# Three token chains laid out anew behind the main loop of a cross-attention, linear-attention and expert kernel

## The chip, the cores and the metric

The kernel runs on one core of one Trainium2 chip. The metric is the device time of one execution in microseconds. An execution under the profiler has its own time, and a span (first to last instruction) a little shorter than that.

## What is computed

The reference has three residual stages over x (8 x 64 tokens of 256), all in float32:

```python
x = x + xattn(layernorm(x), ctx)   # 16 heads of 64 over 1601 context rows, layernorm inside, tanh gate
x = x + attn(layernorm(x))         # linear attention, 8 heads of 64, batches of 64 tokens
x = x + ffn(layernorm(x))          # router, top 2 of 8 experts, 256 -> 1024 (relu) -> 256
# attn:
q = softmax(q, axis=-2) * SCALE    # over the 64 features of a head
k = softmax(k, axis=-1)
context = einsum('bhdn,bhen->bhde', k, v)
out = einsum('bhde,bhdn->bhen', context, q)
```

(In the code the 64 tokens of a batch are regrouped by the reshape of the reference, so that both softmaxes are over groups of 64 within a token's 512 columns.)

## The kernel before, in words

The 512 tokens are 4 tiles of 128 (MT). Every engine has its own queue with a program written out by hand; semaphores tie them together. The work runs in "slots" numbered k. Slots 0 to 207 (NSLOT = 16 groups x 13 context tiles) are the cross-attention: in slot k TensorE makes the scores of tile k (`scores`, L1491), and `times_context` (L1515, 12 matmuls) of tile k - 19. VectorE subtracts the maximum from tile k - 17 (L1073) and makes the low part of tile k - 18 (L1098); ScalarE takes exponents and high parts (L839). The last tiles of that pipeline run out in slots 208 to 226, and the last attention group is written to `oT` in slot 230. `DRAIN` is 231.

Behind that each token tile m goes through a "chain" (one function `chain(m, o)` for each engine, L882, L1145, L1601) of 16 steps o. On TensorE: 0 output product O (`wout_sb`), 2 transpose T1, 3 K, 4 Q, 5 V, 6 and 7 transposes KT and QT, 8 and 9 the head contexts C0 and C1, 10 OT, 11 Y, 13 transpose T2, 14 router product R. On VectorE: 0 adds and statistics (to `eps1`), 1 ln1, 3 K minus its maximum, 4 the same for Q and the normalisation of k, 6 the normalisation of q, 9 cbd, 11 adds and statistics (to `eps2`), 12 ln2, 13 lnT_lo, 14 the routing group (logit, top, tdiff, index, topf, two onehot, cnt), 15 the gates. ScalarE copies and exponentiates between them. POOL makes each `rstd` (L732), in an order written out at L767.

`CHAIN_AT` gives the slot in which a chain starts. In each slot, on each engine, the odd chains come first, then the slot's own work, then the even chains (L1752 to L1758, the same on the others). Chains 0 and 2 use PSUM bank `trp[0]`, chain 1 `trp[1]`, chain 3 a bank of `scp`. The buffers of a chain (`ln_out`, `lnT`, `ke`, `qe`, `kn`, `v_sb`, `cbd`) exist twice, set m % 2; so chain 2 waits for chain 0's logit, chain 3 for chain 1's (L1621).

The chains that aren't done at `SPREAD` = 239 leave only chain 3, whose steps 8 to 14 are set by `LAST` between the tiles of the first expert: n = 0 to 7 are `h_tile(0, n)` (6 matmuls each, L1711), n = 8 to 15 `y_tile(0, n - 8)` (4 matmuls each, L1726). After n = 1 come the ranks of chains 0 to 2 (`first_ranks`, L1738), at the end `last_rank`, which needs chain 3's cnt; then the second half of the tokens. ScalarE writes the high parts of the expert weights (`high_weights`, in quarters: two of w1, two of w2), POOL the low parts (`low_weights`, L735, L743): `w_ready` counts them; the first h tile needs two of them, the first y tile four. SP loads the raw weights, the first two experts when the last `times_context` is done.

Of the kernel before, what the change touches and what calls it, by code (L numbers as in the profile page):

```python
# [125 lines left out]
def build(nc, x, ctx_n, ctx_t, gamma, beta, w_q, w_kt, w_v, w_out, b_out, gate, Wq, Wk, Wv, Wo, bo,  # L126
          W_router, b_router, W1, b1, W2, b2, out):
    with ExitStack() as es:
# [91 lines left out]
        lqT = ke  # L220
        lo_T = qe[:].rearrange("p r (t q) -> p r t q", q=P)
# [74 lines left out]
        w2_sp = tsb("w2_sp", [P, 2, FT, 2 * D], F32R)  # L296
# [139 lines left out]
        def chain_bank(m):  # L436

            return [trp[0], trp[1], trp[0], scp[:, MT - 1, :]][m]
# [13 lines left out]
        def w_quarter(s, part):  # L452

            if part < DT:
                return w1_raw[:, s, part, :], w1_hi[:, s, part, :], w1_lo[:, s, part, :]
            fs = slice((part - DT) * FT // 2, (part - DT + 1) * FT // 2)
            return w2_raw[:, s, fs, :], w2_sp[:, s, fs, 0:D], w2_sp[:, s, fs, D:2 * D]
# [225 lines left out]
        def _(pool):  # L683
# [83 lines left out]
            for m, which in ((0, 1), (1, 1), (0, 2), (2, 1), (1, 2), (3, 1), (2, 2)):  # L767
                chain_rstd(m, which)
# [26 lines left out]
        def _(act):  # L795
# [86 lines left out]
            def chain(m, o):  # L882

                r, bank = m % 2, chain_bank(m)

                def after_pe(name):
                    act.wait_ge(chain_pe[m], PE_NO[name])

                def after_dve(name):
                    act.wait_ge(chain_dve[m], DVE_NO[name])  # L890

                if o == 2:
                    after_pe("T1")
                    act.activation(lnT[:, r, :, :], bank[:, 0:D].rearrange("p (t q) -> p t q", q=P),
                                   ACT.Copy).then_inc(chain_act[m], 1)
                elif o == 4:
                    after_dve("ksub")
                    act.activation(ke[:, r, :, :], ke[:, r, :, :], ACT.Exp).then_inc(chain_act[m], 1)
                elif o == 5:
                    after_dve("qsub")  # L900
                    act.activation(qe[:, r, :], qe[:, r, :], ACT.Exp).then_inc(chain_act[m], 1)
                    after_pe("V")
                    act.activation(v_sb[:, r, :], bank, ACT.Copy).then_inc(chain_act[m], 1)
                elif o == 6:
                    after_pe("KT")
                    act.activation(kn[:, r, :], bank, ACT.Copy).then_inc(chain_act[m], 1)
                elif o == 7:
                    after_pe("QT")
                    act.activation(lqT[:, r, :, :].rearrange("p t q -> p (t q)"), bank,
                                   ACT.Copy).then_inc(chain_act[m], 1)  # L910
                elif o == 10:
                    after_pe("OT")
                    act.activation(lo_T[:, r, :, :].rearrange("p t q -> p (t q)"), bank,
                                   ACT.Copy).then_inc(chain_act[m], 1)
                elif o == 13:
                    after_pe("T2")
                    ps = bank[:, 0:D].rearrange("p (t q) -> p t q", q=P)
                    if m == 0:
                        act.wait_ge(split_ok, len(JOBS))
                    act.activation(lnT_hi[:, :, m * P:(m + 1) * P], ps, ACT.Copy).then_inc(chain_act[m], 1)  # L920
                    act.activation(lnT[:, r, :, :], ps, ACT.Copy).then_inc(chain_act[m], 1)
# [84 lines left out]
        def _(dve):  # L1006
# [138 lines left out]
            def chain(m, o):  # L1145

                r, bank = m % 2, chain_bank(m)
# [22 lines left out]
                def normalised(which):  # L1170
                    dve.wait_ge(chain_pool[m], which)
                    dst = ln_out[:, r, :] if which == 1 else xln[:, m, :]
                    done(dve.tensor_scalar(dst, x_m, mv[:, m, 0:1], rstd[:, m:m + 1], ALU.subtract, ALU.mult))
# [18 lines left out]
                ke_m = ke[:, r, :, :].rearrange("p t q -> p (t q)")  # L1192
                if o == 0:
                    after_pe("O")
                    done(dve.tensor_tensor(ln_out[:, r, :], bank[:, 0:D], bout_b[:], ALU.add))
                    after("o+b")
                    done(dve.scalar_tensor_tensor(out=x_m, in0=ln_out[:, r, :], scalar=tg[:, 1:2], in1=x_m,
# [7 lines left out]
                elif o == 4:  # L1205
                    after_pe("Q")
                    minus_row_max(1, qe[:, r, :], "qmax")
                    after_act("exp_k")
                    normalise(0, ke_m, "ksum", "krec")
                elif o == 6:  # L1210
                    after_act("exp_q")
                    normalise(1, qe[:, r, :], "qsum", "qrec")
                elif o == 9:
                    after_pe("C1")
                    done(dve.tensor_scalar(cbd[:, r, :, :, :], bank.rearrange("p (b t e) -> p b t e", b=2, e=LD),
                                           float(LD) ** -0.5, None, ALU.mult))
                elif o == 11:
                    after_pe("Y")
                    done(dve.tensor_tensor(ln_out[:, r, :], bank[:, 0:D], bo_b[:], ALU.add))
                    after("y+b")  # L1220
                    done(dve.tensor_tensor(x_m, x_m, ln_out[:, r, :], ALU.add))
# [224 lines left out]
        def _(pe):  # L1446
# [154 lines left out]
            def chain(m, o):  # L1601

                r, bank = m % 2, chain_bank(m)
# [11 lines left out]
                if o == 0:  # L1615
                    pe.wait_ge(o_ok, 4 * (m + 1))
                    if m < 2:
                        pe.wait_ge(out_ok, NSLOT)
                        pe.wait_ge(max_ok, NSLOT)
                    else:  # L1620
                        pe.wait_ge(chain_dve[m - 2], DVE_NO["logit"])  # L1621
# [4 lines left out]
                elif o == 2:  # L1626
                    after_dve("ln1")
                    for dt in range(DT):
                        ins = pe.transpose(bank[:, dt * P:(dt + 1) * P], ln_out[:, r, dt * P:(dt + 1) * P], ident[:])
                    done(ins)  # L1630
                elif o == 3:
# [3 lines left out]
                    for t in range(HP):  # L1635
                        for dt in range(DT):
                            ins = pe.matmul(bank[:, t * P:(t + 1) * P], lw_sb[:, 1, dt, t * P:(t + 1) * P],
                                            lnT[:, r, dt, :], start=dt == 0, stop=dt == DT - 1)
                    done(ins)
                elif o in (4, 5):  # L1640
                    after_dve("ksub" if o == 4 else "qsub")
                    for dt in range(DT):
                        ins = pe.matmul(bank, lnT[:, r, dt, :], lw_sb[:, 0 if o == 4 else 2, dt, :],
                                        start=dt == 0, stop=dt == DT - 1)
                    done(ins)
                elif o == 6:
                    after_act("v")
                    after_dve("kmul")
                    for t in range(HP):
                        ins = pe.transpose(bank[:, t * P:(t + 1) * P], ke[:, r, t, :], ident[:])  # L1650
                    done(ins)
                elif o == 7:
                    after_act("kn")
                    after_dve("qmul")
                    for t in range(HP):
                        ins = pe.transpose(bank[:, t * P:(t + 1) * P], qe[:, r, t * P:(t + 1) * P], ident[:])
                    done(ins)
                elif o in (8, 9):
# [7 lines left out]
                    for t in range(HP):  # L1666
                        for hr in head_rows:
                            h = slice(t * P + hr.start, t * P + hr.stop)
                            n0 = (b * HP + t) * LD
                            ins = pe.matmul(bank[hr, n0:n0 + LD], kn[rows, r, h], v_sb[rows, r, h],  # L1670
                                            start=True, stop=True)
                    done(ins)
                elif o == 10:
                    after_dve("cbd")
                    for t in range(HP):
                        for b in range(2):
                            for hr in head_rows:
                                ins = pe.matmul(bank[hr, t * P + b * Q:t * P + (b + 1) * Q], cbd[hr, r, b, t, :],
                                                lqT[hr, r, t, b * Q:(b + 1) * Q], start=True, stop=True)
                    done(ins)  # L1680
                elif o == 11:
                    after_act("lo_T")
                    for t in range(HP):
                        ins = pe.matmul(bank[:, 0:D], lo_T[:, r, t, :], wo_sb[:, t, :],
# [7 lines left out]
                elif o == 14:  # L1692
                    after_act("lnT2")
                    after_dve("lnT_lo")
                    for dt in range(DT):
                        ins = pe.matmul(bank[:, 0:NE], lnT[:, r, dt, :], wr_sb[:, dt, :],
# [19 lines left out]
            def y_tile(p, f):  # L1716
# [7 lines left out]
                for m in tiles(p):  # L1724
                    ms = slice(m * P, (m + 1) * P)
                    pe.matmul(scp[:, m, :], h_hi[:, f, ms], w2_sp[:, 0, f, :], start=f == 0, stop=False)  # L1726
                    ins = pe.matmul(scp[:, m, 0:D], h_lo[:, f, ms], w2_sp[:, 0, f, 0:D],
# [98 lines left out]
            def y_z(z, f):  # L1826
# [12 lines left out]
                for a in range(2):  # L1839
                    b = 2 * (z % 2) + a  # L1840
                    ms = slice(a * P, (a + 1) * P)
                    pe.matmul(scp[:, b, :], h_hi[:, f, ms], w2_sp[:, s, f, :], start=f == 0, stop=False)  # L1842
                    ins = pe.matmul(scp[:, b, 0:D], h_lo[:, f, ms], w2_sp[:, s, f, 0:D],  # L1843
# [24 lines left out]
            for a in range(2):  # L1868
                b = 2 * (z % 2) + a
                ms = slice(a * P, (a + 1) * P)  # L1870
                for f in range(FT):
                    if a == 0:
                        pe.wait_ge(hl_ok, (z + 2) * FT + (f + 1))
                    pe.matmul(scp[:, b, :], h_hi[:, f, ms], w2_sp[:, s, f, :], start=f == 0, stop=False)
                    ins = pe.matmul(scp[:, b, 0:D], h_lo[:, f, ms], w2_sp[:, s, f, 0:D],
# [68 lines left out]
```

## Time and profile before

| | us |
|---|---|
| median of 3 runs | 940.38 (939.36 to 943.42) |
| the profiled execution | 947.82 |
| its span | 946.0 |
| PE busy | 902.2 (95%) |
| DVE busy | 700.6 (74%) |
| POOL busy | 603.3 (64%) |
| ACT busy | 520.4 (55%) |

PE is TensorE's matmuls, DVE VectorE, ACT ScalarE, POOL GpSimd. Busy time is the time in which the engine has an instruction under way. The slots from 208 on begin near 663 us of the span, the first h tile at 768.7, the last rank at 794.2. The clock column of a row is TensorE's granted clock as a share of full speed. Durations of matmuls overlap: the start of one matmul comes before the end of the one before, so the cost of a row of matmuls is read from start to start.

### The profile page before, as it was taken

How to read it: one execution, taken by the hardware profiler on the slowest of the kernel's cores; microseconds unless marked ns; L12 is line 12 of the kernel's file. 1: busy time of each engine (PE TensorE's matmuls, PEld its weight loads, DVE VectorE, ACT ScalarE, POOL GpSimd, SP SyncE). 2: the span in 40 equal slices, each digit the busy share in tenths (PEclk: the TensorE clock that was granted, in tenths of full speed). 3: DMA queues.
4: the chain of work that ended last, by engine and by line, in shares of the span. 5: the costliest groups of instructions: out<-in, count | busy, mean ns of one | idle time of the engine just before them, and what ended most of it. 6: DMA issues, size and time to landing. Idle time of an engine off the chain costs nothing.

```text
span 946.0 us, 17135 instructions
## 1 busy us (share of the span) xinstructions
PE 902.2 (95%) x6228; PEld 787.7 (83%) x6228; DVE 700.6 (74%) x1223; ACT 520.4 (55%) x915; POOL 603.3 (64%) x647
## 2 busy tenths in 40 slices
PE   6999999999999999999999999999999889999997
PEld 3567888888888888888888888888878668998996
DVE  4659787887978878797786879777586576866765
ACT  2547565565655665565565655655354233565662
POOL 5739778857957876895795789471001056677773
PEclk9999999999999999999999999999999978999998
DMA  5872222312322331332231122110200521466632
GB/s 166 258 261 74 76 78 83 95 43 81 89 55 79 88 86 56 81 85 59 77 84 48 46 60 65 40 37 2 67 1 2 178 87 51 138 219 208 225 123 78
DMA packets 102802, 88.23 MB, mean 93 GB/s; under 512 B 10032, under 2 KB 98112, under 8 KB 102720
## 3 DMA queue, kind: packets, MB, share of 16 engines
q1 hardware_dynamic: 101952, 85.04, 29.9%
q0 software_dynamic: 768, 2.10, 0.7%
q8 instruction: 51, 0.84, 0.4%
q14 instruction: 31, 0.25, 0.1%
HBM read 67.46 MB, written 19.66 MB: 92 GB/s over the span
## 4 chain that ended last, share of the span: by engine, by line
PE 82%; DVE 11%; ACT 3%; issue 2%; POOL 1%; DMA 1%; SPq 0%; POOLq 0%; DVEq 0%; ACTq 0%
PE sps L1510 29%; PE scp L1528 10%; PE scp L1530 9%; PE scp L1529 9%; PE scp L1842 3%; DVE u_sb L1108 2%; PE sps L1821 2%; PE wps L1821 2%; PE wps L1555 2%; PE scp L1843 2%; DVE st L1073 1%; PE sps L1623 1%; PE scp L1478 1%; PE sps L1464 1%; DVE pt_lo L1098 1%
## 5 line engine op out<-in xcount | busy, mean ns | idle before, releaser
L1528 PE MATMUL scp<-cn,pt_hi 128*128 128x258 f32 (+1 forms) x832 | 239.4, 288 | 4.4 <-DVE pt_lo L1098 3.7
L1529 PE MATMUL scp<-cn,pt_hi 128*128 128x256 f32 (+1 forms) x832 | 234.9, 282 | 0.0
L1530 PE MATMUL scp<-cn,pt_lo 128*128 128x258 f32 (+1 forms) x832 | 234.7, 282 | 0.0
L837 ACT ACTIVATE st<-sps 128x512 f32<-128x512 f32 (+1 forms) x208 | 123.4, 593 | 146.5 <-PE sps L1510 145.8
L1098 DVE TENSOR_TENSOR pt_lo<-st,pt_hi 128x512 fp32r<-128x512 f32 (+1 forms) x208 | 195.3, 939 | 6.6 <-ACT pt_hi L846 6.6
L1073 DVE TENSOR_TENSOR st<-st,mbc 128x512 f32<-128x512 f32 (+1 forms) x208 | 158.1, 760 | 39.0 <-ACT mbc L860 38.4
L843 ACT ACTIVATE st<-st 128x512 f32<-128x512 f32 (+1 forms) x208 | 130.3, 627 | 89.2 <-DVE st L1073 88.6
L1510 PE MATMUL sps<-qk_hi,ct_hi 128*128 128x512 f32 (+1 forms) x416 | 168.2, 404 | 11.1 <-DVE cmax L1084 6.6
L1528 PEld LDWEIGHTS scp<-cn,pt_hi 128*128 128x128 f32 (+1 forms) x832 | 156.9, 189 | 14.9 <-DVE pt_lo L1098 6.6
L1510 PE MATMUL sps<-qk_hi,ct_lo 128*128 128x512 f32 (+1 forms) x416 | 164.2, 395 | 0.0
L1510 PE MATMUL sps<-qk_lo,ct_hi 128*128 128x512 f32 (+1 forms) x416 | 163.4, 393 | 0.0
L1529 PEld LDWEIGHTS scp<-cn,pt_hi 128*128 128x128 f32 (+1 forms) x832 | 157.2, 189 | 7.4 <-issue 0.2
L1084 DVE TENSOR_TENSOR cmax<-cmax,sps 128x512 f32<-128x512 f32 x192 | 130.6, 680 | 37.3 <-ACT st L837 37.2
L1530 PEld LDWEIGHTS scp<-cn,pt_lo 128*128 128x128 f32 (+1 forms) x832 | 157.7, 190 | 0.0
L707 POOL TENSOR_TENSOR cn<-raw,zero 128x256 fp32r<-128x256 f32 (+1 forms) x104 | 79.9, 768 | 118.1 <-PE scp L1530 111.9
L846 ACT ACTIVATE pt_hi<-st 128x512 fp32r<-128x512 f32 (+1 forms) x208 | 131.5, 632 | 6.6
L709 POOL TENSOR_TENSOR cn<-raw,cn 128x256 fp32r<-128x256 f32 (+1 forms) x104 | 100.3, 964 | 8.2
L1510 PEld LDWEIGHTS sps<-qk_hi,ct_hi 128*128 128x128 f32 (+1 forms) x416 | 76.6, 184 | 30.9 <-issue 15.8
L709 POOL TENSOR_TENSOR ct_lo<-raw,ct_hi 128x256 fp32r<-128x256 f32 (+1 forms) x104 | 92.9, 893 | 8.1
L1510 PEld LDWEIGHTS sps<-qk_hi,ct_lo 128*128 128x128 f32 (+1 forms) x416 | 76.4, 184 | 20.3
L707 POOL TENSOR_TENSOR ct_hi<-raw,zero 128x256 fp32r<-128x256 f32 (+1 forms) x104 | 85.5, 822 | 11.8 <-DMA raw<-ctx_t 11.8
L1510 PEld LDWEIGHTS sps<-qk_lo,ct_hi 128*128 128x128 f32 (+1 forms) x416 | 76.6, 184 | 10.3
(291 smaller groups left out, 1496.3 us busy)
## 6 DMA issues: line engine op xcount, KB each, us to landing
w_raw<-W SPq DMA_DIRECT2D x22, 1024.0 KB, 7.6
raw<-ctx_t SPq DMA_DIRECT2D x96, 128.0 KB, 2.2
raw<-ctx_n SPq DMA_DIRECT2D x96, 128.0 KB, 2.0
raw<-qk_scratch SPq DMA_DIRECT2D x56, 128.0 KB, 2.0
xg_scratch<-zrow SPq DMA_DIRECT2D x32, 128.0 KB, 2.3
yg_scratch<-zrow SPq DMA_DIRECT2D x32, 128.0 KB, 2.3
qk_scratch<-stage_b SPq DMA_DIRECT2D x4, 896.0 KB, 4.8
qk_scratch<-stage_a SPq DMA_DIRECT2D x4, 896.0 KB, 4.5
```

The source lines that it names most:

```text
L707: pool.tensor_tensor(hi, src, z.broadcast_to(tuple(src.shape)), ALU.add).then_inc(split_hi, 1)
L709: pool.tensor_tensor(lo, src, hi.bitcast(F32), ALU.subtract).then_inc(done, 1)
L837: act.activation(st[0:rows(j), par, j, :], sps[0:rows(j), u % 2, :], ACT.Copy).then_inc(out_ok, 1)
L843: act.activation(p, p, ACT.Exp).then_inc(exp_ok, 1)
L846: act.activation(pt_hi[0:rows(j), r, :], p, ACT.Copy).then_inc(hi_ok, 1)
L1073: dve.tensor_tensor(p, p, mbc[0:rows(j), par, :], ALU.subtract).then_inc(sub_ok, 1)
L1084: dve.tensor_tensor(m, m, src, ALU.max).then_inc(max_ok, 1)
L1098: dve.tensor_tensor(pt_lo[0:rows(j), r, :], st[0:rows(j), par, j, :], pt_hi[0:rows(j), r, :].bitcast(F32), ALU.subtract).then_inc(lo_ok, 1)
L1510: ins = pe.matmul(sps[0:rows(j), u % 2, :], a[:, dt, cols], v[:, par, dt, :], start=c == 0, stop=c == 5)
L1528: pe.matmul(scp[:, t, 0:D + 2], hi, cn[0:rows(j), j, 0:D + 2], start=j == 0, stop=False)
L1529: pe.matmul(scp[:, t, 0:D], hi, cn[0:rows(j), j, D + 2:CNW], start=False, stop=False)
L1530: ins = pe.matmul(scp[:, t, 0:D + 2], lo, cn[0:rows(j), j, 0:D + 2], start=False, stop=j == SJ - 1)
```

## The change

Chain 1 starts at slot 223 in place of 213, chain 2 at 224 in place of 223; chain 3 stays at 231. `SPREAD` becomes 240, so step 8 of chain 3 (C0) runs in slot 239, ahead of the first h tile, and no longer behind the second. Chain 3 gets a third set of buffers, laid where `w2_sp` of expert 1 lies; chain 2 keeps set 0. ScalarE writes the high parts of that expert's `w2` later, and those of its `w1` at n = 4 and 12 in place of 2 and 6. `W_HI_AT` moves from 234 to 235 with SPREAD.

```diff
-CHAIN_AT = [NSLOT, NSLOT + 5, NSLOT + 15, DRAIN]
+CHAIN_AT = [NSLOT, NSLOT + 15, NSLOT + 16, DRAIN]
+CHAIN_SET = [0, 1, 0, 2]
 CHAIN_LEN = 16
 SPREAD = CHAIN_AT[2] + CHAIN_LEN
-LAST = dict(zip((1, 2, 4, 5, 6, 11, 13), range(SPREAD - DRAIN, CHAIN_LEN - 1)))
+LAST = dict(zip((2, 4, 5, 6, 11, 13), range(SPREAD - DRAIN, CHAIN_LEN - 1)))
...
-        w2_sp = tsb("w2_sp", [P, 2, FT, 2 * D], F32R)
+        w2_sp = [tsb("w2_sp0", [P, FT, 2 * D], F32R)]
+        third = ExitStack()
...
+        ln_out3 = third_sb("ln_out3", [P, D])
+        lnT3 = third_sb("lnT3", [P, DT, P])
+        ke3 = third_sb("ke3", [P, HP, P])
+        qe3 = third_sb("qe3", [P, HID])
+        kn3 = third_sb("kn3", [P, HID])
+        v_sb3 = third_sb("v_sb3", [P, HID])
+        cbd3 = third_sb("cbd3", [P, 2, HP, LD])
+        third.close()
+        w2_sp.append(tsb("w2_sp1", [P, FT, 2 * D], F32R))
+
+        def three(two, last):
+            return [two[:, 0], two[:, 1], last[:]]
...
-            for m, which in ((0, 1), (1, 1), (0, 2), (2, 1), (1, 2), (3, 1), (2, 2)):
+            for m, which in ((0, 1), (0, 2), (1, 1), (2, 1), (3, 1), (1, 2), (2, 2)):
                 chain_rstd(m, which)
...
-                r, bank = m % 2, chain_bank(m)
+                r, bank = CHAIN_SET[m], chain_bank(m)
...
-                if n % 4 == 2:
-                    high_weights(1, n // 4)
+                if n in (4, 12):
+                    high_weights(1, n // 8)
             chain(MT - 1, 15)
+            act.wait_ge(chain_pe[MT - 1], PE_NO["R"])
             for f in range(FT):
                 relu(1, f)
+                if f in (2, 5):
+                    high_weights(1, 2 + f // 3)
...
                     if m < 2:
                         pe.wait_ge(out_ok, NSLOT)
                         pe.wait_ge(max_ok, NSLOT)
-                    else:
-                        pe.wait_ge(chain_dve[m - 2], DVE_NO["logit"])
+                    elif m == 2:
+                        pe.wait_ge(chain_dve[0], DVE_NO["logit"])
```

The other lines of the diff only replace a buffer's index `[:, r]` by the list of three, `ke_of[r]` and so on, and `w2_sp[:, s]` by `w2_sp[s]`.

## Rows read from the trace of the kernel before

**Rows 1.** Busy time by stretch: us, PE, PEld, DVE, ACT, POOL, clock, DMA, GB/s

```profile
664.00:723.00 59.00, 55.42 (x484) 47.64 (x483) 41.73 (x90) 27.77 (x50) 2.82 (x3) 1.00 0.07 25
...
745.00:768.70 23.70, 17.75 (x130) 13.26 (x129) 12.40 (x30) 8.36 (x13) 8.70 (x13) 0.89 0.05 16
...
757.00:766.90 9.90, 6.77 (x26) 3.63 (x24) 8.06 (x15) 4.53 (x8) 6.35 (x10) 1.00 0.00 0
```

**Rows 2.** PE's order of time: start, us, line, tiles, count, idle before and releaser

```profile
718.20 0.51 PE L1696 MATMUL sps<-wr_sb,lnT 128*128 128x8 f32 x4
...
721.26 3.62 PE L1623 MATMUL sps<-wout_sb,oT 128*128 128x256 f32 x16
...
733.06 1.95 PE L1637 MATMUL sps<-lnT,lw_sb 128*128 128x128 f32 x16
...
740.08 1.98 PE L1643 MATMUL sps<-lw_sb,lnT 128*128 128x512 f32 x4 [1.51 <-DVE qe L1181]
...
745.00 3.62 PE L1623 MATMUL scp<-wout_sb,oT 128*128 128x256 f32 x16
748.55 1.43 PE L1670 MATMUL sps<-v_sb,kn 64*64 64x64 f32 x32
...
752.20 1.15 PE L1678 MATMUL sps<-ke,cbd 64*64 64x64 f32 x32 [0.16 <-DVE cbd L1215]
753.28 3.68 PE L1637 MATMUL scp<-lnT,lw_sb 128*128 128x128 f32 x16
756.79 1.89 PE L1684 MATMUL sps<-wo_sb,qe 128*128 128x256 f32 x8
```

**Rows 3.** DVE's order of time, 737 to 774 us: step starts, routing group, gates

```profile
737.39 0.36 DVE L1244 TENSOR_SCALAR onehot<-eidx,topf 128x8 f32<-128x8 f32 x2
...
738.61 0.69 DVE L1179 TENSOR_REDUCE lmax<-sps 128x8 f32<-128x512 f32 x1 [0.65 <-PE sps L1643]
...
741.50 0.15 DVE L1249 TENSOR_SCALAR tsum<-texp 128x1 f32<-128x1 f32 x1
...
748.66 0.42 DVE L1195 TENSOR_TENSOR ln_out<-scp,bout_b 128x256 f32<-128x256 f32 x1 [3.93 <-PE scp L1623]
...
750.32 0.15 DVE L1168 TENSOR_SCALAR mv<-mv 128x1 f32<-128x1 f32 x1
...
767.76 0.16 DVE L1234 TENSOR_TENSOR logit<-sps,br_b 128x8 f32<-128x8 f32 x1
...
769.17 1.35 DVE L1244 TENSOR_SCALAR onehot<-eidx,topf 128x8 f32<-128x8 f32 x2
...
771.13 0.14 DVE L1249 TENSOR_SCALAR tsum<-texp 128x1 f32<-128x1 f32 x1
...
773.45 0.41 DVE L1268 CAST h_hi<-sps 128x256 fp32r<-128x256 f32 x1
```

**Rows 4.** POOL's order of time, 750 to 773 us: rstd and the first low parts

```profile
750.55 0.55 POOL L732 TENSOR_TENSOR rstd<-mv,mhalf 128x1 f32<-128x1 f32 x1 [20.56 <-DVE mv L1168]
...
761.27 6.01 POOL L743 TENSOR_TENSOR w_lo<-w_raw,w_hi 128x256 fp32r<-128x256 f32 x8
```

**Rows 5.** DVE's order of time: the two normalising multiplies, and x's low part

```profile
762.76 1.15 DVE L1189 TENSOR_TENSOR ke<-ke,lrec 128x512 f32<-128x512 f32 x1
...
767.15 0.69 DVE L1189 TENSOR_TENSOR qe<-qe,lrec 128x512 f32<-128x512 f32 x1
...
809.60 0.68 DVE L1365 TENSOR_TENSOR lnT_lo<-sps,lnT_hi 128x512 fp32r<-128x512 f32 x1
```

**Rows 6.** Busy time by stretch of 1 us, at the edges of the lower clock

```profile
753.00:754.00 1.00, 1.00 (x15) 0.93 (x12) 0.00 (x0) 0.60 (x2) 0.00 (x0) 0.65 0.00 0
...
780.00:781.00 1.00, 1.00 (x14) 0.78 (x15) 0.93 (x4) 0.23 (x1) 0.00 (x0) 0.69 0.65 205
```

**Rows 7.** The chain that ended last: one h tile at either clock

```profile
769.08 1.28 PE sps L1711 x6
...
784.50 0.71 PE wps L1711 x6
```

More of the change, by code:

```diff
@@ L295, in build, with third_sb @@
         w1_lo = tsb("w1_lo", [P, 2, DT, FF], F32R)
-        w2_sp = tsb("w2_sp", [P, 2, FT, 2 * D], F32R)
+        w2_sp = [tsb("w2_sp0", [P, FT, 2 * D], F32R)]
+        third = ExitStack()
+        def third_sb(name, shape):
+            return third.enter_context(nc.sbuf_tensor(name, shape, F32))
+        ln_out3 = third_sb("ln_out3", [P, D])
[9 more added lines that the diff above has]
+            return [two[:, 0], two[:, 1], last[:]]
+        ln_out_of, lnT_of, ke_of, qe_of = three(ln_out, ln_out3), three(lnT, lnT3), three(ke, ke3), three(qe, qe3)
+        kn_of, v_sb_of, cbd_of = three(kn, kn3), three(v_sb, v_sb3), three(cbd, cbd3)
+        lqT_of, lo_T_of = ke_of, [q.rearrange("p (t q) -> p t q", q=P) for q in qe_of]
         w1_raw = tsb("w1_raw", [P, 2, DT, FF])
@@ L1171, in normalised @@
                     dve.wait_ge(chain_pool[m], which)
-                    dst = ln_out[:, r, :] if which == 1 else xln[:, m, :]
+                    dst = ln_out_of[r][:, :] if which == 1 else xln[:, m, :]
                     done(dve.tensor_scalar(dst, x_m, mv[:, m, 0:1], rstd[:, m:m + 1], ALU.subtract, ALU.mult))
@@ L1190, in normalise @@
                                            lrec[:, m, w, :].unsqueeze(2).broadcast_to((P, LH, LD)), ALU.mult))
-                ke_m = ke[:, r, :, :].rearrange("p t q -> p (t q)")
+                ke_m = ke_of[r][:, :, :].rearrange("p t q -> p (t q)")
                 if o == 0:
                     after_pe("O")
-                    done(dve.tensor_tensor(ln_out[:, r, :], bank[:, 0:D], bout_b[:], ALU.add))
+                    done(dve.tensor_tensor(ln_out_of[r][:, :], bank[:, 0:D], bout_b[:], ALU.add))
                     after("o+b")
-                    done(dve.scalar_tensor_tensor(out=x_m, in0=ln_out[:, r, :], scalar=tg[:, 1:2], in1=x_m,
+                    done(dve.scalar_tensor_tensor(out=x_m, in0=ln_out_of[r][:, :], scalar=tg[:, 1:2], in1=x_m,
                                                   op0=ALU.mult, op1=ALU.add))
@@ L1218, in chain @@
                     after_pe("Y")
-                    done(dve.tensor_tensor(ln_out[:, r, :], bank[:, 0:D], bo_b[:], ALU.add))
+                    done(dve.tensor_tensor(ln_out_of[r][:, :], bank[:, 0:D], bo_b[:], ALU.add))
                     after("y+b")
-                    done(dve.tensor_tensor(x_m, x_m, ln_out[:, r, :], ALU.add))
+                    done(dve.tensor_tensor(x_m, x_m, ln_out_of[r][:, :], ALU.add))
                     norm_stats("x2", "stats2", "aggr2")
@@ L1628, in chain @@
                     for dt in range(DT):
[L1629 removed]
+                        ins = pe.transpose(bank[:, dt * P:(dt + 1) * P], ln_out_of[r][:, dt * P:(dt + 1) * P], ident[:])
                     done(ins)
@@ L1725, in y_tile @@
                     ms = slice(m * P, (m + 1) * P)
-                    pe.matmul(scp[:, m, :], h_hi[:, f, ms], w2_sp[:, 0, f, :], start=f == 0, stop=False)
-                    ins = pe.matmul(scp[:, m, 0:D], h_lo[:, f, ms], w2_sp[:, 0, f, 0:D],
+                    pe.matmul(scp[:, m, :], h_hi[:, f, ms], w2_sp[0][:, f, :], start=f == 0, stop=False)
+                    ins = pe.matmul(scp[:, m, 0:D], h_lo[:, f, ms], w2_sp[0][:, f, 0:D],
                                     start=False, stop=f == FT - 1)
@@ L1841, in y_z @@
                     ms = slice(a * P, (a + 1) * P)
-                    pe.matmul(scp[:, b, :], h_hi[:, f, ms], w2_sp[:, s, f, :], start=f == 0, stop=False)
-                    ins = pe.matmul(scp[:, b, 0:D], h_lo[:, f, ms], w2_sp[:, s, f, 0:D],
+                    pe.matmul(scp[:, b, :], h_hi[:, f, ms], w2_sp[s][:, f, :], start=f == 0, stop=False)
+                    ins = pe.matmul(scp[:, b, 0:D], h_lo[:, f, ms], w2_sp[s][:, f, 0:D],
                                     start=False, stop=f == FT - 1)
```

52 lines of the change are left out of this document (25 added, 27 removed).

## The prediction

> **What bounds the kernel now.** The page shows TensorE busy nearly everywhere; the weak place is the stretch behind the loop, so I read that stretch only: busy time by stretch first, then the order of time on each engine. From 664 to 723 us (slots 208 to 222, chains 0 and 1 beside the last `times_context`) TensorE is busy 55.4 of 59.0 us; from 745.0 to 768.7 (chain 3 beside the end of chain 2) it is busy only 17.8 of 23.7 [rows 1]. There the chain itself is the bound: each step of one engine waits for the step before on another. Slots are positions in the queues, not times; what a chain step costs is the hand-over plus whatever stands ahead of it on its engine.
>
> **The move out of slots 213 to 222.** Chain 1 starts at slot 223 now, so its steps 0 to 9 leave this stretch. On TensorE these are the output product 3.6, K 1.8, Q and V 1.9 each, the two C products 0.6 each (half of the 1.43 for two), and three transposes, about 1 together: 11.4 us [rows 2]. On VectorE the norm step (1.7 us from its first to its last instruction), the K step 1.3, the Q step with the normalisation of k 2.9, the q normalisation 1.5, the cbd scaling 0.7 go too [rows 3]. I replayed the slots, each instruction starting at the later of its engine's turn and its releaser, with the trace's durations. Until slot 212 nothing differs. From there the terms are: `times_context` 1.44 us a slot, two VectorE passes of 0.6 for each slot (subtract, low part), chain 0's steps. The router product of chain 0 comes at 708.9 instead of 718.2 [rows 2]. So 9.3 of the 11.4 us come free; 2 us turn into waits for `pt_lo`, since chain 0 alone leaves TensorE one short wait where VectorE's x2 and norm steps run (near 704) and one near 715 behind chain 1's own norm step.
>
> **The slots 223 to 230.** Chain 1's steps 0 to 7 now share these with chain 2's 0 to 6. Chain 1's output product (3.6 us, slot 223) stands ahead of chain 2's (slot 224), whose start comes at about 717.4 against 721.3 [rows 2]: 3.9 us earlier. From there VectorE and TensorE take turns for two chains: K1, Q1 with 2.9 us of VectorE behind it, K2, V1, Q2 with 2.9 us again, KT1, V2, QT1, KT2. This takes as long as before (two chains cover each other, where before chain 2 had slots 227 to 230 nearly alone and chain 1's tail stood ahead of it), and chain 3's output product starts at about 741.1 against 745.0 [rows 2]: still 3.9 us ahead.
>
> **The slots 231 to 239.** Three chains share them: chain 1's steps 8 to 15, chain 2's 7 to 15, chain 3's 0 to 8. Chain 3 is the latest, so its path sets the end. Output product to 744.7; norm step 1.7 and rstd on POOL 0.6 [rows 3, 4], ln1 done 747.55. T1 waits for OT of chain 1 (1.15), so 748.4; then C1 of chain 2 0.6 and Y of chain 1 1.8 stand ahead of K: K runs 750.9 to 752.85 (before, mostly at half clock, it took 3.7 instead of 1.95 [rows 2]; I take it at full clock, as TensorE has no hole of 3 us ahead of it any more). VectorE's K step until 754.3; Q until 756.4; the Q step until 759.3. Before, the q normalisation of chain 3 came soon behind that. Now VectorE's queue holds ahead of it chain 2's x2 and statistics (1.7, to 761.0), chain 1's lnT_lo, chain 2's ln2 (0.4 each, like ln_out's instruction of the same 256 columns [rows 3], with its wait for rstd until 762.1) and chain 1's whole group of routing instructions, logit to cnt.
>
> That group is the term with two prices. Next to an idle POOL its two one-hots take 0.36 us together; with POOL in its weight split they take 1.35, and the group takes 3.37 us from logit to the next instruction [rows 3] (about 1.4 next to an idle POOL, where its first seven parts take as long and only the rest differ). POOL starts its split as soon as chain 2's second rstd is done, at 761.7 by the replay, against 761.27 before [rows 4], so it runs beside the group: I take 3.4, the nearest row, and keep 1.4 for the range. Then: group to 765.5, q normalisation to 767.1, QT 767.2 to 767.65, its copy to 768.4, C0 at 768.5, and the first product of the expert at 769.1 against 768.73. The 3.9 us are gone. What is left is C0 of chain 3, which moves from behind the second expert product (at half clock 1.05) to ahead of the first, and the ranks, which wait for cnt of chain 2: chain 1's gates 2.3 (771.13 to 773.45 before [rows 3]) and chain 2's group 3.4 give 773.0. The ranks end at about 774.4 instead of 775.2. **Sum here: 0.8 us saved.**
>
> One sentence of the Trainium skill bears on that group: GPSIMD Engine Reference, section Key points, says that GpSimd contends with VectorE instructions in a two-port mode or with two SBUF inputs. By this rule the q normalisation's multiply (two SBUF inputs) would be slowed too; the trace has one such multiply at 1.15 us and the next, of the same form and also beside POOL, at 0.69 [rows 5], so it agrees half of the time, and by the rule the sum would lose some 0.5 us more.
>
> **The rest.** POOL's rstd order is changed to the new order of the chains; none waits longer. The SP queue issues the weights when `pv_ok` is full, some 7 us earlier; nothing else is on the queue then. The high parts of `w2` of expert 1 are written by ScalarE between the second pass's relus 2 and 5, 1.05 us each: relu 3 comes 0.6 late, VectorE's splits behind it are back to back, so x's low part (VectorE, 809.60 before [rows 5]) ends 0.6 later, at 810.9, where its user started at 810.8: 0.15 us. If that cover of 0.5 us were gone, it would cost 0.6. POOL's low parts need them at 804 and 806.8, ScalarE has them at about 803 and 805.3: nothing. The third set itself costs nothing: it lies where `w2_sp` of expert 1 comes later, and chain 3's wait for chain 1's logit goes.
>
> Sum: 0.8 - 0.15 = 0.65 us less, from a span of 946.0 and an own time of 947.82 to 947.2. The profiled execution is 7.4 us above the median of the runs (940.38); I take the difference from the median: **939.7**. My replay has some forty hand-overs good to 0.05 us each, all of one sign at worst: 2 us either way.
>
> **Clock.** TensorE was granted half clock (1.2 of 2.4 GHz) from 753.35 to 756.6 and from 767 to 780.3 [rows 6]; ahead of the second it was busy 6.8 of 9.9 us [rows 1], with gaps. By the replay it is emptier there now: between 760.0 and 769.1 it has R, KT, T2, QT, R and C0, together some 2.5 us. I take the same fall and the same length. An expert product of six matmuls takes 1.28 at half and 0.71 at full clock [rows 7].
>
> **The rivals.**
> A, POOL as the new bound, smaller gain: the routing group is not slowed. Then h starts when POOL has two parts of `w1` (762.0 + 6.0 [rows 4] = 768.0), 0.7 earlier than before, C0 out of the way: in all 2.8 us saved with the ranks, 937.7. For it: the fast rows 3; against: POOL starts just there.
> B, the clock is kept: the fall near 767 doesn't come or ends after the first products. Five products save 2.85, C1 0.45, ranks about 1.2: 4.5 more than the sum, 935.2. For it: the denser stretch 745 to 759; against: the hole behind it.
> C, slower: the fall comes earlier and the rise later, because the hole before the first expert product is 9 us long. Place: 763 to 787. Price: QT, R, C0 0.5, then products 5 to 7 1.7, Y 1.7, and the first three y tiles 1.2: 5.1, less the 0.65: 944.8. It decides from the point at which TensorE is at half clock beyond 784. A first fall in slots 213 to 222, where the two waits of 1.6 us are, would add 1.7.
> D, the change doesn't do what it says: the queues wait for the same producers and chain 3 starts at 745 as before, because o_ok of the last group sets it. By the trace the last `times_context` ends at 733.1 and the transposes behind it are within the queue, so it isn't set by anything outside: a small chance; 3.9 us worse than my sum, 943.6.
>
> **How the numbers follow.** My forecast 0.46, A 0.20, B 0.17, C 0.12, D 0.05. About 0.5% (4.7 us) is what a measurement of this kernel can tell from no change; the runs before spread over 4 us. Faster by more: B (0.17) and a little of A, 0.20. Slower by more: most of C and a little of D, 0.12. The rest 0.68. The range takes in A, D and the two us of the replay, and runs from within B to within C: 933.5 to 944.5. My forecast with A alone would run from 936.5 to 941.5.
>
> **What would show it.** Right: chain 3's output product 3 to 5 us earlier than 745.0; its K 1.9 us; VectorE in chain 1's routing group (one-hots above 1 us for both) when QT of chain 3 waits; the first L1711 product (by its new line) near 769; TensorE busy under 4 us from 760 to 769; what is left of the gain at 795 is left at the end. Wrong: a first expert product before 767 or after 771; half clock shorter than 8 us or longer than 17 behind it; a chain 0 router product not near 709.

## The result, and the profile after

| | before | after |
|---|---|---|
| median of 20 runs each, us | 941.23 | 945.38 |
| ratio, 95% interval | | 1.0031 [1.0016, 1.0046] |
| the profiled execution | 947.82 | 947.1 |
| its span | 946.0 | 945.3 |

The change costs 0.31%, about 2.9 us. (The ratio is that of the means, 944.60 and 941.64 us; the medians lie 4.2 us apart, as the runs of each kernel spread over 6 to 7 us.) Two more measurements, told below, gave 1.0023 and 1.0024. The three weighted by their intervals give 1.0027 [1.0017, 1.0038]. The two profiled executions contradict this: after's is 0.7 us *shorter*. Why spans mislead here comes up in the experiments. The head of the page after:

```profile
span 945.3 us, 17135 instructions
...
PE 901.1 (95%) x6228; PEld 786.9 (83%) x6228; DVE 703.4 (74%) x1223; ACT 520.1 (55%) x915; POOL 602.2 (64%) x647
```

Busy times hardly moved, as the same work is done. The order of time on PE of the changed kernel shows the new layout (columns: start, us, line, count, idle before and releaser; it answers to [rows 2]):

```profile
709.43 0.58 PE L1720 MATMUL sps<-wr_sb,lnT 128*128 128x8 f32 x4
...
741.80 3.72 PE L1647 MATMUL scp<-wout_sb,oT 128*128 128x256 f32 x16
...
751.91 1.95 PE L1661 MATMUL scp<-lnT,lw_sb 128*128 128x128 f32 x16
...
755.37 1.98 PE L1667 MATMUL scp<-lw_sb,lnT 128*128 128x512 f32 x4 [0.43 <-DVE ke L1205]
...
759.13 1.88 PE L1667 MATMUL scp<-lw_sb,lnT 128*128 128x512 f32 x4
762.50 0.58 PE L1720 MATMUL sps<-wr_sb,lnT 128*128 128x8 f32 x4 [1.49 <-DVE lnT_lo L1254]
762.94 0.64 PE L1674 MATMUL scp<-ident,ke 128*128 128x128 f32 x4
763.41 0.38 PE L1714 MATMUL sps<-ident,xln 128*128 128x128 f32 x2
768.47 1.09 PE L1680 MATMUL scp<-ident,qe 128*128 128x128 f32 x4 [4.68 <-DVE qe L1213]
769.35 0.86 PE L1720 MATMUL sps<-wr_sb,lnT 128*128 128x8 f32 x4
770.25 1.12 PE L1694 MATMUL scp<-v_sb,kn 64*64 64x64 f32 x16
771.29 0.58 PE L1735 MATMUL sps<-lnT_hi,w_hi 128*128 128x256 f32 x1
```

Chain 3's output product (741.80) is 3.2 us ahead of before, its K product runs at full clock, its V product starts at 759.13. Then TensorE has nothing to do but some 1.3 us of small work (762.50 to 763.79) until QT at 768.47: the row says 4.68 us of idle time, ended by VectorE's `qe` multiply. The first h tile starts at 771.29, before at 768.73. VectorE's order of time in that hole (it answers to [rows 3, 5]):

```profile
761.94 0.42 DVE L1254 TENSOR_TENSOR lnT_lo<-sps,lnT_hi 128x256 fp32r<-128x256 f32 x1
762.68 0.41 DVE L1197 TENSOR_SCALAR xln<-x_sb,mv,rstd 128x256 f32<-128x256 f32 x1 [0.33 <-POOL rstd L753]
763.12 0.17 DVE L1258 TENSOR_TENSOR logit<-sps,br_b 128x8 f32<-128x8 f32 x1
...
764.43 1.34 DVE L1268 TENSOR_SCALAR onehot<-eidx,topf 128x8 f32<-128x8 f32 x2
765.80 0.64 DVE L1270 TENSOR_TENSOR cnt<-onehot 128x8 f32<-128x8 f32 x1
766.36 0.67 DVE L1209 TENSOR_REDUCE lsum<-qe 128x8 f32<-128x512 f32 x1
...
767.31 1.02 DVE L1213 TENSOR_TENSOR qe<-qe,lrec 128x512 f32<-128x512 f32 x1
```

VectorE rests for only 0.33 us: chain 1's and chain 2's work stands ahead of chain 3's q normalisation (766.36). The routing group takes 3.24 us, from 763.12. POOL's order of time shows what runs beside it (it answers to [rows 4]):

```profile
762.82 6.09 POOL L764 TENSOR_TENSOR w_lo<-w_raw,w_hi 128x256 fp32r<-128x256 f32 x8
```

The q multiply takes 1.02 us, against 0.69 for the same one in [rows 5]. The Trainium skill (GPSIMD Engine Reference, Key points) says that GpSimd contends with a VectorE instruction that has two SBUF inputs; on this row the trace agrees. The 0.69 of [rows 5] is a weak case against it: that multiply started at 767.15, 0.08 us ahead of POOL's next group of splits (767.23), and so it was, by 0.08 to 0.10 us and with the same 0.69, in e3, e5, f3, g2 and h1 below. But g1 has 0.69 well inside such a group, so the price isn't fixed.

TensorE's clock, busy time by stretch of after (PE, PEld, DVE, ACT, POOL, clock; it answers to [rows 6]):

```profile
766.00:767.00 1.00, 0.00 (x0) 0.00 (x0) 1.00 (x2) 0.00 (x0) 1.00 (x2) 0.85 0.00 0
...
783.00:784.00 1.00, 1.00 (x19) 0.88 (x16) 0.60 (x2) 0.09 (x1) 0.21 (x1) 0.62 0.00 0
```

The fall to half clock comes inside the hole: 0.85 in its slice of 1 us puts it at 766.7, and 0.62 puts the rise at 783.8, so it lasts 17.1 us. Read in the same way, [rows 6] give 767.0 to 780.6 for the kernel before, 13.7 us, and not the end at 780.3 that the prediction has. The earlier fall of before (753.3 to 756.7) is gone.

**Two theories** came out of this. T, the queue: the head start is lost, because VectorE's queue puts two other chains' work, slowed by POOL, ahead of chain 3's q normalisation. K, the clock: the hole brings half clock earlier and for longer, and that is the cost. A third suspect, W, is what else changed: the third buffer set and the late high parts of `w2`.

### The profile page after: what moved, and what is told of

Its sections match the earlier page's. It is cut to its first block, busy times and chain, and to the rows that moved or that the text cites. A ratio compares the mean times of both kernels' runs of the same rounds, so it can differ in the third digit from the quotient of the medians.

```text
span 945.3 us, 17135 instructions
## 1 busy us (share of the span) xinstructions
PE 901.1 (95%) x6228; PEld 786.9 (83%) x6228; DVE 703.4 (74%) x1223; ACT 520.1 (55%) x915; POOL 602.2 (64%) x647
## 4 chain that ended last, share of the span: by engine, by line
PE 82%; DVE 11%; ACT 3%; issue 2%; POOL 1%; DMA 1%; SPq 0%; POOLq 0%; DVEq 0%; ACTq 0%
PE sps L1534 29%; PE scp L1552 10%; PE scp L1554 9%; PE scp L1553 9%; PE scp L1866 3%; DVE u_sb L1132 2%; PE sps L1845 2%; PE wps L1845 2%; PE wps L1579 2%; PE scp L1867 2%; DVE st L1097 1%; PE sps L1647 1%; DVE pt_lo L1122 1%; PE scp L1502 1%; PE sps L1488 1%
## 5 line engine op out<-in xcount | busy, mean ns | idle before, releaser
L1534 PEld LDWEIGHTS sps<-qk_hi,ct_hi 128*128 128x128 f32 (+1 forms) x416 | 76.7, 184 | 31.1 <-issue 15.9
```

Source lines behind the costliest of these rows:

```text
L1534: ins = pe.matmul(sps[0:rows(j), u % 2, :], a[:, dt, cols], v[:, par, dt, :], start=c == 0, stop=c == 5)
```

## The experiments

The kernels of one group share a chip and the runs of the kernel before: e1, e3, e4 and e5 ran on the chip called 3; f1, f2, f3 and e6 on 11; g1 and g2 on 13; h1 and h2 on 8. Ratios are used, since the kernel before itself has medians of 941.1 to 946.5 us on these chips. Each run also lists its mean granted clock, so its **half-clock time** is estimated as (1 - clock) x 2 x span; the clock is listed to 0.001, which is 1 us either way of it. Within a group the time rises by 0.31 to 0.41 us with each us of it, and a fit over the group's runs gives each kernel's difference to the kernel before **at equal half-clock time**. The mean half-clock times themselves scatter widely: for 12 runs against 23 or 35, a difference is good to 2.4 to 4 us either way.

**e1, VectorE's order.** Gates of chains 1 and 2 wait behind the eighth h tile's split; chain 3's q normalisation comes ahead of chain 1's routing group.

```diff
 for k in range(NSLOT, SPREAD):
     for m in chains_in(k, 1):
-        chain(m, k - CHAIN_AT[m])
+        if m == 3 or k - CHAIN_AT[m] < 14:
+            chain(m, k - CHAIN_AT[m])
...
+    if k == CHAIN_AT[1] + 14:
+        chain(1, 14)
...
+    if n == FT - 1:
+        chain(1, 15)
+        chain(2, 15)
```

> The changed kernel with VectorE's queue alone put in another order: in slot 237 chain 3's q normalisation and chain 2's lnT_lo come ahead of chain 1's routing group, and the gates of chains 1 and 2 come behind the eighth h tile. Theory T (the loss is chain 3's q normalisation waiting on VectorE behind chain 1's routing group, which POOL slows): chain 3's QT starts near 765.5 instead of 768.5 us, the first h tile near 769 (then held by POOL's low parts) instead of 771.3, the time falls by 2 to 3 us, to 942.4 to 943.4. Rival K (the loss is only the longer stretch at half clock, 16.8 instead of 13.3 us) and rival W (the loss is the later high parts of w2 and the third set): the tiles start earlier but the time stays within 1 us of 945.4.

Ratio 1.0015 [0.9995, 1.0036], at equal half-clock time +1.3 (0.8 either way). The order of time on PE of this kernel:

```profile
764.76 0.63 PE L1687 MATMUL scp<-ident,qe 128*128 128x128 f32 x4 [1.27 <-DVE qe L1213]
...
790.41 0.58 PE L1727 MATMUL scp<-wr_sb,lnT 128*128 128x8 f32 x4 [1.21 <-DVE lnT_lo L1254]
```

The hole of 4.68 us is 1.27. But the first h tile then waits 0.88 us for POOL's `w_lo` (768.67), and the gates that I moved now stand ahead of chain 3's `lnT_lo` and make its router product wait 1.21 us. T is right about the hole; my order only moved part of the wait. The time doesn't decide: 1.0015 is what T expected, but the interval holds K's expectation too.

**e3, the layout back.** The changed kernel with the slots, `LAST` and the rstd order of before; third set, late `w2` and no wait for logit kept.

```diff
-CHAIN_AT = [NSLOT, NSLOT + 15, NSLOT + 16, DRAIN]
+CHAIN_AT = [NSLOT, NSLOT + 5, NSLOT + 15, DRAIN]
```

> The changed kernel with the slots of before (chain 1 at 213, chain 2 at 223, C0 of chain 3 behind the second h tile, the old order of rstd), but with the third set and the late high parts of w2. T: the loss goes with the slots, so 941.2 plus 0.15, between 940.5 and 942.5. W: the loss stays, 944 to 946. K: no number of its own; the half-clock stretch should be that of before.

Ratio 1.0006 [0.9981, 1.003], at equal half-clock time +0.2 (0.8). The third suspect is cleared to that accuracy: what costs is the layout.

**e4 and e5, TensorE kept busy.** Dummy 128x512 matmuls in the slots around the hole, one ahead of slot 237 and four ahead of 238 in the changed kernel (e4), one ahead of each of slots 236 to 238 in the kernel before (e5, whose edit is shown).

```diff
+def keep_busy(n):
+    for _ in range(n):
+        pe.matmul(up, ident[:], lw_sb[:, 0, 0, :], start=True, stop=True)
 for k in range(NSLOT, SPREAD):
+    keep_busy({236: 1, 237: 1, 238: 1}.get(k, 0))
```

> The changed kernel with five matmuls of 128x512 on a free bank, which nothing reads, in TensorE's hole ahead of chain 3's QT (one ahead of slot 237, four ahead of slot 238; 0.98 us each at full clock). If the hole is what lets the clock fall and the fill keeps it: the h tiles take 0.71 us instead of 1.28, the time falls by 4 to 6 us, to 939 to 941. T expects the hole's length itself unchanged (QT still near 768.5) and a first h tile near 770.5. K expects the whole loss and more to go with the clock. If the fill does not keep the clock: 945 to 946.5.

> The kernel before with three such matmuls, one ahead of each of the slots 236, 237 and 238, in the three holes of 1 to 1.5 us ahead of its first h tile. If they keep the clock there: 4 us less, near 937. If not: within 1 us of 941.2, since the holes are as long as the fill. K and T differ only in what they make of the pair with the filled changed kernel: by T the filled changed kernel stays about 1 to 2 us behind this one, by K it is level or ahead.

One such matmul holds TensorE for 0.9 us. e4: 1.0036 [1.0015, 1.0057]. Its mean half-clock time is that of the kernel before (21.3 against 21.1 us), but at equal half-clock time it costs +4.0 (0.8). In its profile the clock is whole until after QT, and falls to half for the first two h tiles all the same (770.96). The fill itself isn't what costs: counted from chain 0's output product, QT starts at 104.0 us as in the changed kernel, and the first h tile at 106.0 in place of 106.8. Part of the 4.0 stands at the end, where this profile has the longest of the stalls told under h2 (ScalarE idle for 6.33 us); the rest is not explained. e5: **0.9975 [0.9952, 0.9998]**, half-clock time 14.1 us against 21.1 (3.7 either way). At equal half-clock time it differs by +0.4 (0.8), so the gain is the clock's. Its first h tile runs at full clock.

**f1, the changed kernel again**, and **e6, POOL's first low parts wait for chain 1's cnt** (one run, for the durations).

```diff
+pool.wait_ge(chain_dve[1], DVE_NO["cnt"])
 for part in range(4):
     low_weights(0, part)
```

> The changed kernel itself, so that it stands on the same chip as the others. Both theories: 0.2 to 0.45% above the kernel before. T (the wait on VectorE's queue): after the half-clock time of each execution is taken out, it is still 1.5 to 2.5 us above the kernel before. K (the clock alone): what is left then is within 0.7 us of nothing.

> The changed kernel with POOL's first low parts waiting for chain 1's cnt, a look at one price: the routing group of chain 1 next to an idle POOL. T with POOL as the cause of its length: the group takes 1.4 instead of 3.2 us, the q normalisation's multiply 0.69 instead of 1.02, QT of chain 3 starts near 766.3 instead of 768.5, and the first h tile then waits for POOL until about 770.8. If the group stays at 3.2 us, POOL is not what slows it.

f1: 1.0023 [1.0002, 1.0044], +1.2 (0.6) at equal half-clock time. So something is lost that isn't the clock, a little less than T expected (1.5 to 2.5). The half-clock time is 19.2 us against 15.9, which at this group's 0.31 us for each would be another 1.0 us. But that difference of 3.3 is good only to 4.0 either way: that the changed kernel loses by the clock too is likely, and not shown. e6's order of time on VectorE, with POOL idle until 764.71:

```profile
763.10 0.17 DVE L1259 TENSOR_TENSOR logit<-sps,br_b 128x8 f32<-128x8 f32 x1
...
764.05 0.36 DVE L1269 TENSOR_SCALAR onehot<-eidx,topf 128x8 f32<-128x8 f32 x2
764.46 0.17 DVE L1271 TENSOR_TENSOR cnt<-onehot 128x8 f32<-128x8 f32 x1
764.54 0.68 DVE L1210 TENSOR_REDUCE lsum<-qe 128x8 f32<-128x512 f32 x1
...
765.49 1.18 DVE L1214 TENSOR_TENSOR qe<-qe,lrec 128x512 f32<-128x512 f32 x1
```

The same routing group takes 1.44 us in place of 3.24: POOL's split costs it 1.8 us. The q multiply runs beside POOL again and takes 1.18, where 0.69 was expected. On PE the price shows at once, since the h tile now waits for the late split:

```profile
766.81 0.85 PE L1681 MATMUL scp<-ident,qe 128*128 128x128 f32 x4 [3.03 <-DVE qe L1214]
...
770.72 0.58 PE L1736 MATMUL sps<-lnT_hi,w_hi 128*128 128x256 f32 x1 [1.26 <-POOL w_lo L764]
```

**f2, order and POOL together.** e1's order, but chain 1's gates behind the eighth h tile and chain 2's behind chain 3's routing group; POOL splits the first quarter of `w1` before chain 2's second rstd.

```diff
-for m, which in (..., (3, 1), (1, 2), (2, 2)):
+for m, which in (..., (3, 1), (1, 2)):
     chain_rstd(m, which)
+low_weights(0, 0)
+chain_rstd(2, 2)
```

> The changed layout with VectorE's order of the earlier experiment (chain 3's q normalisation ahead of chain 1's routing group; chain 1's gates behind the eighth h tile, chain 2's behind chain 3's routing group), and POOL splits the first quarter of w1 ahead of chain 2's second rstd. T: first h tile near 767 us, R of chain 3 no longer late; at equal half-clock time 2 to 4 us below the changed kernel and 1 to 2 below the kernel before, ratio 0.997 to 1.000. K: as the changed kernel, ratio 1.002 to 1.004, unless its half-clock time differs.

Ratio 1.0014 [0.9999, 1.003]; at equal half-clock time **-0.8 (0.6)**, so it loses less than the kernel before in waits, and 2.0 (0.8) less than f1. This is the test of T: with the order and the split mended, what the changed kernel loses beside the clock is gone. On PE:

```profile
765.28 1.09 PE L1689 MATMUL scp<-ident,qe 128*128 128x128 f32 x4 [1.11 <-DVE qe L1215]
766.16 0.86 PE L1729 MATMUL sps<-wr_sb,lnT 128*128 128x8 f32 x4
767.20 1.12 PE L1703 MATMUL scp<-v_sb,kn 64*64 64x64 f32 x16 [0.18 <-ACT ke L932]
768.25 0.58 PE L1744 MATMUL sps<-lnT_hi,w_hi 128*128 128x256 f32 x1
```

No long hole is left, and still QT takes 1.09 us, its half-clock duration, and the mean half-clock time is 22.7 us against 15.9 (3.5 either way). T's part is undone; the clock, at 0.31 us for each of these 6.9, is what keeps this kernel at 1.0014. The gain in waits is spent there: 1.0014 can't be told from f1's 1.0023.

**f3, chain 1 at slot 218, chain 2 at 223**, half of the move (with `LAST` and the rstd order of before).

```diff
-CHAIN_AT = [NSLOT, NSLOT + 15, NSLOT + 16, DRAIN]
+CHAIN_AT = [NSLOT, NSLOT + 10, NSLOT + 15, DRAIN]
```

> A size between: chain 1 at slot 218 (five later than before, five earlier than in the change), chain 2 at 223, all else as in the changed kernel (third set, late w2), C0 of chain 3 behind the second h tile. T: chain 1's routing group is over in slot 232, ahead of chain 3's critical steps, so nothing of the loss: first h tile 767 to 769, ratio 0.997 to 1.001. If instead any delay of chain 1 costs (it fills TensorE's waits best at 213): ratio near 1.0015.

Ratio 1.0068 [1.0042, 1.0094], +4.3 (0.7) at equal half-clock time; the expectation was wrong. Its order of time on PE:

```profile
728.11 0.63 PE L1680 MATMUL sps<-ident,qe 128*128 128x128 f32 x4 [1.68 <-DVE qe L1213]
...
735.69 3.62 PE L1661 MATMUL sps<-lnT,lw_sb 128*128 128x128 f32 x16
...
752.50 1.68 PE L1647 MATMUL scp<-wout_sb,oT 128*128 128x256 f32 x7
```

The loss is all ahead of chain 3: the clock is at half from 730.0 to 740.3 (chain 2's K product takes 3.62 us for 1.95), and chain 3 starts at 752.5, 7.5 us later than before. From there to the first h tile (776.49) it takes 24.0 us, before 23.7, with no idle time above 1.9 us, as T has it. The wait of 1.68 us ahead of QT can't be all of the cause of the fall, since before has one of 1.59 us there (729.64) and no fall behind it. I take it that chain 1's tail and chain 2's head cover each other badly in slots 227 to 232; no run shows it.

**g1, f2 with e5's three matmuls; g2, e5 again on another chip.**

> The kernel with VectorE's order mended and POOL's first split early, and now one dummy 128x512 matmul on TensorE ahead of each of the steps at slots 236, 237 and 238. Order theory plus clock theory: mended order alone was 1 us faster than the kernel before at equal half-clock time (935.1 against 936.1) but spent 22.7 us at half clock against 15.9, and so came out at ratio 1.0014; if three small matmuls do here what they did in the kernel before (half-clock time down by 7 us), the ratio is 0.996 to 0.998, the first expert product is at 768.3 to 769, at full clock, and mean half-clock time is below 17 us. Rival: the filling only helps where the hole is short; the half-clock time stays above 20 us and the three matmuls cost 1 us: ratio 1.001 to 1.003.

> The kernel before with one dummy 128x512 matmul on TensorE ahead of each of the steps at slots 236, 237 and 238, once more on another chip. If the earlier gain (ratio 0.9975, half-clock time 14.1 against 21.1 us) belongs to the filling, the ratio is 0.996 to 0.999 and the mean half-clock time 4 us or more below that of the kernel before. If it was the chip's or the hour's, the ratio is 1.000 to 1.001 and the half-clock times are alike.

g1: 1.0006 [0.9986, 1.0026], between the two expectations; +0.9 (0.6) at equal half-clock time, which is 21.7 us against 22.3. Against the kernel before on its chip, then, it has no more half-clock time, where f2 had 6.9 us more, but it has lost f2's gain in waits. In its profile the clock is whole where it was wanted, but TensorE then stands still:

```profile
764.00:770.00 6.00, 5.07 (x47) 3.97 (x47) 5.62 (x15) 4.25 (x8) 5.46 (x9) 1.00 0.01 3
770.00:776.00 6.00, 3.37 (x36) 3.04 (x35) 5.13 (x14) 1.35 (x4) 3.33 (x5) 0.91 0.25 53
```

In the second stretch PE's order of time has the next wait, of the ranks for chain 2's cnt; on VectorE this stands behind two slowed routing groups in a row (766.37 to 773.28):

```profile
773.41 0.61 PE L1768 MATMUL scp<-cnt,all_ones 128*128 128x8 f32 x4 [2.63 <-DVE cnt L1272]
```

g2: 0.9986 [0.9966, 1.0006], half-clock time 18.6 against 22.3 us (3.9 either way). e5 and g2 are the same kernel; weighted together they give 0.9981 [0.9966, 0.9996]. That is the one version here that is faster than both kernels, by 0.2%, and its interval nearly reaches 1.

**h1, the kernel before; h2, the changed kernel**, one more chip, each profiled once more.

> The kernel before, profiled once more. In the profiles so far ScalarE's second y_hi (near 937 us) stands 2.4 to 3.9 us behind the matmuls that it waits for, for nothing the trace shows, in all six profiles of the chips called 3 and 13 and in the first profile of the kernel before, and in none of the four of chip 11 nor in the changed kernel's. If the stall belongs to the chip or its session, this profile and that of the changed kernel in the same call agree: both have it or neither. If it belongs to the kernel, this one has it and the changed kernel has not. Ratio 1.000 within 0.0015; QT of chain 3 no wait above 1.5 us; half clock behind the first expert product at most 14 us.

> The changed kernel a third time, beside the kernel before. Theory (2 us lost in the stretch to the first expert product and behind it, whatever the chip does at the end): first expert product 2 to 3 us later than in the profile of the kernel before of this call, with a hole of 4.7 us ahead of QT, ratio 1.002 to 1.004. Rival (the loss of 2.9 us in the medians was largely the end's, a matter of the chip): ratio within 0.001 of 1. ScalarE's second y_hi: late here if late in the profile of the kernel before of this call.

h1: 1.0003 [0.9981, 1.0024]. h2: 1.0024 [1.0003, 1.0046], +1.5 (0.7) at equal half-clock time. In h2 half-clock time is 24.9 us against 22.9 (3.5 either way), again no clear difference. The two profiles settle how to read the spans. Counted from chain 0's output product (664.4 in the profile before), the profiles give (e1, e4, e5 and f3 are left out):

| us from chain 0's output product | chain 3's output product | first h tile | first transposes of x | end | the last two apart |
|---|---|---|---|---|---|
| before | 80.6 | 104.4 | 143.9 | 281.6 | 137.7 |
| h1, the same | 80.7 | 104.4 | 144.0 | 281.8 | 137.8 |
| after | 77.3 | 106.8 | 145.8 | 280.8 | 135.0 |
| f1, the same | 77.3 | 106.8 | 145.6 | 280.7 | 135.1 |
| h2, the same | 77.4 | 106.8 | 140.8 | 278.6 | 137.7 |
| e3 | 80.6 | 104.0 | 140.1 | 278.3 | 138.2 |
| f2 | 77.3 | 103.7 | 142.9 | 277.9 | 135.0 |
| g1 | 77.3 | 103.0 | 140.9 | 280.6 | 139.7 |
| g2 | 80.6 | 104.0 | 139.8 | 279.5 | 139.7 |

Up to the first h tile a kernel repeats itself within 0.1 us: the change gains 3.3 us at chain 3's start and is 2.4 us behind at the first h tile, every time. Between there and x's transposes the clock decides: after and f1 stay at half clock for 17.1 us around the first h tile, h2 from 764.0 to 774.3 only, and it gains 5 us on them. This is one and the same kernel. The last column lies near 135, 138 or 139.7. In h2's order of time on ScalarE, and in before's:

```profile
934.21 0.38 ACT L1023 ACTIVATE y_hi<-scp 128x256 fp32r<-128x256 f32 x1 [4.91 <-remote]
```

```profile
937.10 0.38 ACT L999 ACTIVATE y_hi<-scp 128x256 fp32r<-128x256 f32 x1 [4.92 <-remote]
```

In after's it is this:

```profile
936.58 0.38 ACT L1023 ACTIVATE y_hi<-scp 128x256 fp32r<-128x256 f32 x1 [2.39 <-PE scp L1899]
```

With "remote" nothing in the trace released it, and the matmuls that it waits for had ended 2.4 us or more before; TensorE then waits 2.3 us in before, and its placement matmuls run at half clock until 941.0. The same kernel has this stall in h2 and not in after and f1. All four profiles of chip 11 lack it and all eight of the chips 3, 13 and 8 have it. So whether it comes goes by chip or session, not by kernel, and the 2.7 us that after's profile gains at the end have nothing to do with the change. How long it is may well depend on the kernel: ScalarE is idle for 4.9 to 5.0 us in before, e1, e3, e5, h1 and h2, and for 5.4 to 6.3 us in e4, g1 and g2, all three with dummy matmuls. What the stall is stays open; no run here shows it.

## Why the prediction was wrong, step by step

The measured +0.31% lies within the 0.5% either way that held 0.68 of the chance, but on the other side of the forecast: 0.65 us were to be saved, and 2.9 were lost.

- **Slots 213 to 222**: right within 0.8 us. Chain 0's router product at 708.9 was forecast; 709.43 came. Chain 2's output product was forecast at 717.4 and came at 718.23. The two waits for `pt_lo` are 1.60 and 1.67 us, against 0.34 and 0.56 before, so they take 2.4 us more, and 2 were forecast.
- **Slots 223 to 230**: right. They take 23.6 us from chain 2's output product to chain 3's, and 23.7 were forecast. Chain 3's came at 741.80 in place of 741.1, so the lead is 3.3 us, not 3.9; what is missing was gone before slot 224.
- **Slots 231 to 239, up to the q normalisation**: the order, the engine and the group that stands ahead were named rightly. K at full clock was right, though the hole of 3 us that was to explain its half clock before isn't in the trace: TensorE's longest idle time there is 1.62 us, ahead of T1 (751.60). The queue slipped by 0.3 more: Q step done 760.3 (forecast 759.3), group done 766.36 (765.5). The group's price of 3.4 was right (3.24), and e6 shows the cause that I assumed (1.44 beside an idle POOL). That only the one-hots and cnt differ was misread: the cast of topi goes from 0.17 to 0.51 us too. Rival A is out, and so is D, by chain 3's start at 741.80.
- **The step that failed** is "q normalisation to 767.1, QT 767.2 to 767.65, its copy to 768.4, C0 at 768.5, and the first product of the expert at 769.1". I priced it as if the clock stayed whole until the expert, although my own clock paragraph put the fall near 767 and rival C named QT, R and C0. The multiply took 1.02 instead of 0.69, QT, R and C0 ran at half clock, and the first h tile came at 771.29: 2.2 us late, 0.7 of it from chain 3's start, 0.6 from the queue and the multiply, 0.9 from there on. The sum had 3.9 us won and 4.3 used up; it was 3.3 won and 5.7 used up, which is 2.4 us behind, in all three profiles of the changed kernel; f2 shows that the queue's order and POOL's split, the two together, are what costs at equal half-clock time (2.0 us).
- **"The same fall, the same length"**: wrong for this profile. The fall is not at the same place relative to the work: it lies ahead of QT by 1.8 us, where before it was 1.0. The stretch is 17.1 us, not 13.7. But h2 has 10.2 us with the same kernel, and over the runs of f1 and h2 the mean half-clock time is longer by 3.3 and 2.0 us, neither clear of its scatter. This part of the loss stays open.
- **The ranks**: forecast to end at 774.4, 0.8 us gained; they ended at 776.43, 1.2 lost. What moved out of their way (C0) had moved ahead of the first tile, where it costs the same 1.04 us from start to start, at half clock too.
- **The late `w2`** at 0.15 us and the third set at nothing: e3 doesn't contradict them (+0.2, 0.8 either way).
- **The rivals**: B is out for the median. C had the right sign and, in part, the right mechanism, at 12%. Its condition was half clock beyond 784, and 783.8 came in the first profile. The time came near its price, but 1.2 to 1.5 us of the loss (f1, h2) stand at equal half-clock time, which C doesn't have; that its number fits is in part luck. Half clock for QT, R and C0 belongs in the forecast itself.
- **The sum** stood on one execution 7.4 us above the median. Its end held a stall and half-clock matmuls that come and go; as a difference the sum didn't suffer from that, but the range around the median was too narrow on the slow side: 945.38 lies above my 944.5, and 0.85 us of that is the median of before itself, 941.23 in the 20 runs.

## What to carry to other kernels

A head start on one engine is worth only what the queue of the next leaves of it: where three chains share a queue written by hand, place the latest chain's step ahead of the earlier chains' leftovers (e1 and f2 took the 4.68 us hole down to 1.3 and 1.1, though f2's shorter waits were spent again at half clock). Price everything behind a hole at the clock that the hole leaves behind. And compare profiles from a common event to a common event, not span with span: here every kernel profiled twice or more repeats within 0.1 us up to the first h tile, while the spans of the changed kernel's three profiles differ by 2.2 us and their last stretches by 2.7.

## What the runs showed of the hardware

- VectorE's smallest instructions suffer most beside POOL: two one-hots of 128x8 take 1.34 us in place of 0.36, cnt 0.64 in place of 0.17, the cast of topi 0.51 in place of 0.17, a 128x512 multiply of two SBUF inputs 0.85 to 1.19 in place of 0.69, but in seven profiles once 0.69 all the same; a 128x512 reduction is not touched (0.67 and 0.68).
- Executions of one kernel differ in half-clock time by up to 26 us (0 to 26.4 in the 23 runs of the kernel before on chip 11), and a us of it costs 0.31 to 0.41 us here. An h tile, which is matmuls alone, loses more: 0.57 of its 1.28 us [rows 7], 0.45 for each us.
- Three dummy matmuls (2.7 us of work in holes of 0.8 to 1.5 us) took 7.0 (3.7 either way) and 3.7 us (3.9) off the mean half-clock time of the kernel before, on two chips. That f2, without a long hole, spends 22.7 us at half clock is not explained by these runs.
